# Attention over 16 heads: the causal mask and the row maximum in one VectorE operation, the copy of the values on ScalarE

## The reference, cut to what matters

```python
K = jnp.einsum('bpd,ihd->biph', x, W_K)            # 16 heads of 64
Q = jnp.einsum('bpd,ihd->biph', x, W_Q)
V = jnp.einsum('bpd,ihd->biph', x, W_V)
scores = jnp.einsum('biph,biqh->biqp', K, Q)
mask = jnp.tril(jnp.ones((q_len, q_len), dtype=bool))
scores = jnp.where(mask[None, None, :, :], scores, NEG_INF)
attn = jax.nn.softmax(scores / np.sqrt(d_head).astype(np.float32), axis=-1)
z = jnp.einsum('biph,biqp->biqh', V, attn)
out = jnp.einsum('bqf,df->bqd', z_flat, W_O)
```

## Time and profile before

| | us |
|---|---|
| median of 3 runs | 565.84 (563.9 to 568.18) |
| the profiled execution, its time | 566.51 |
| its span in the profile | 564.7 |

### The profile page before, as it was taken

How to read it: one execution, slowest core, us unless ns; L and a number is a source line. 1 busy time by engine, 2 the same in 40 slices (tenths; PEclk the granted TensorE clock), 3 DMA queues, 4 the chain that set the end, 5 groups by cost and what they waited for, 6 DMA issues and landing times.

```text
span 564.7 us, 10428 instructions
## 1 busy us (share of the span) xinstructions
PE 461.5 (82%) x3500; PEld 362.5 (64%) x3500; DVE 374.8 (66%) x1091; ACT 228.8 (41%) x835; POOL 235.9 (42%) x245
## 2 busy tenths in 40 slices
PE   3957895715989179999999999999999997419993
PEld 2324554614989046777787877878787785319993
DVE  6598976851666347767768687696777955345772
ACT  2720001501444006555646466366564564104451
POOL 5002784471444314433435334363444624322453
PEclk9987998555999669999999999999999999758998
DMA  8999600034464200000000000000000000116560
GB/s 296 403 422 420 277 1 1 15 109 136 142 176 148 77 1 2 1 1 2 1 1 2 2 1 11 11 20 1 2 11 11 21 0 1 39 62 178 155 201 19
DMA packets 21878, 47.73 MB, mean 85 GB/s; under 512 B 3233, under 2 KB 13480, under 8 KB 19394
## 3 DMA queue, kind: packets, MB, share of 16 engines
q1 hardware_dynamic: 18818, 40.73, 20.7%
q0 software_dynamic: 3008, 6.34, 3.3%
HBM read 23.82 MB, written 24.15 MB: 85 GB/s over the span
## 4 chain that ended last, share of the span: by engine, by line
PE 69%; DVE 10%; POOL 8%; DMA 5%; issue 5%; ACT 2%; POOLq 0%; SPq 0%; ACTq 0%; DVEq 0%
PE ps L888 10%; PE ps L917 9%; PE ps L964 8%; PE ps L951 7%; PE ps L833 7%; PE ps L846 6%; PE ps L905 5%; PE ps L895 5%; PE ps L923 3%; POOL sum L441 3%; DMA pv<-in_w 2%; POOL sorted_in L466 2%; PE ps L681 2%; POOL sum L445 2%; PE ps L787 1%
## 5 line engine op out<-in xcount | busy, mean ns | idle before, releaser
L495 POOL TENSOR_TENSOR vT<-vT,prec 128x256 f32<-128x256 f32 (+1 forms) x128 | 103.1, 825 | 157.5 <-DVE prec L1373 157.4
L632 ACT ACTIVATE vT<-ps,nmax 128x128 f32<-128x128 f32 (+1 forms) x256 | 105.1, 434 | 27.8 <-DVE nmax L1365 27.8
L640 ACT COPY prod<-ps 128x384 f32<-128x384 f32 x96 | 42.9, 481 | 111.3 <-PE ps L951 108.3
L1365 DVE TENSOR_REDUCE nmax<-ps 128x2 f32<-128x256 f32 (+1 forms) x128 | 62.3, 548 | 25.6 <-PE ps L923 25.6
L888 PE MATMUL ps<-xnT,wb 128*128 128x256 f32 x256 | 67.9, 389 | 4.6 <-DVE xnT L1345 3.9
L951 PEld LDWEIGHTS ps<-cst,vT 128*128 128x128 f32 x384 | 44.7, 140 | 18.8 <-issue 14.5
L632 ACT ACTIVATION_READ_ACCUMULATOR vT<-ps,nmax 128x1 f32 x256 | 55.9, 218 | 0.0
L951 PE MATMUL ps<-cst,vT 128*128 128x128 f32 x384 | 52.5, 273 | 1.8 <-POOL vT L495 1.7
L888 PEld LDWEIGHTS ps<-xnT,wb 128*128 128x128 f32 x256 | 44.8, 195 | 10.8 <-DVE xnT L1345 4.3
L917 PE MATMUL ps<-qk 64*128 64x128 f32 (+1 forms) x512 | 51.2, 339 | 0.0
L964 PE MATMUL ps<-prod 128*64 128x256 f32 (+1 forms) x512 | 50.0, 338 | 1.4 <-ACT prod L640 1.4
(11 more groups left out here) (152 smaller groups left out, 829.8 us busy)
## 6 DMA issues: line engine op xcount, KB each, us to landing
sorted_in<-zero SPq DMA_DIRECT2D x1, 16512.0 KB, 59.2
pv<-in_w SPq DMA_DIRECT2D x30, 259.0 KB, 2.8
pv<-sorted_in SPq DMA_DIRECT2D x46, 129.0 KB, 2.5
wps<-in_w SPq DMA_DIRECT2D x1, 2072.0 KB, 10.1
w2s<-in_w SPq DMA_DIRECT2D x1, 2048.0 KB, 13.8
wb<-in_w_b SPq DMA_DIRECT2D x1, 1536.0 KB, 18.0
xres<-in_x SPq DMA_DIRECT2D x4, 256.0 KB, 3.6
xres<-after_ffn SPq DMA_DIRECT2D x4, 256.0 KB, 3.8
```

Of the source, the lines that this page charges most:

```text
L495: last = nc.gpsimd.tensor_tensor(px, px, view(prec, m_at(n, x) + t * 2, [[1, 2], [0, (t + 1) * P]]), ALU.mult)
L632: last = nc.scalar.activation(pb[:, o:o + (t + 1) * P], wide[:, c:c + (t + 1) * P], ACT.Exp, bias=nmax[:, m:m + 1], accum_out=psum[:, m:m ...
L640: nc.scalar.copy(pT[:, c:c + BLOCKS * P], bank[hh][:, 0:BLOCKS * P]).then_inc(b_pa, 1)
L1365: last = nc.vector.tensor_reduce(nmax[:, m:m + 2], view(wide, x * 1024 + t * P, [[512, 2], [1, (t + 1) * P]]), AX.X, ALU.max, negate=True)
```

## The change

The mask matmuls and their bf16 constants go. VectorE's reductions become eight fused operations, `tensor_tensor_reduce`: each reads one score block from PSUM and the mask from `cst` in SBUF, writes -(scores + mask) back in place and gives the minimum of that, which is `nmax`. The exponential reads with scale -1. The mask has a block of zeros (`C_OPEN`) ahead of its triangle (`C_CAUSAL`), so that one piece of 256 columns serves `t = 1`. `b_s` now counts once for a step, behind the scores of both pairs, and VectorE waits for it ahead of `invert(n, 1)`. `copy_v` goes from VectorE to ScalarE, between `copy_p(n, 1, 1)` and `exp_b(n1, 1)`. VectorE's `copy_p` stands ahead of the last fused operation, and `copy_qk(n2, 0)` ahead of the last four.

```diff
@@ constants @@
-C_ID, C_BEFORE, C_CAUSAL, C_FIRST, C_UPTO = 0, 128, 256, 384, 392
+C_ID, C_BEFORE, C_OPEN, C_CAUSAL, C_FIRST, C_UPTO = 0, 128, 256, 384, 512, 520
@@ ScalarE @@
-            nc.scalar.copy(id_bf[:], ident)
...
-            nc.scalar.copy(causal[:], cst[:, C_CAUSAL:C_CAUSAL + P]).then_inc(in_r, 1)
...
-                                                    bias=nmax[:, m:m + 1], accum_out=psum[:, m:m + 1])
+                                                    bias=nmax[:, m:m + 1], scale=-1.0, accum_out=psum[:, m:m + 1])
...
+            def copy_v(n, i):
+                act.wait_ge(b_vp, nth(n) + 3)
+                c = (i % 2 * HB + i // 2 * 8) * DHB
+                nc.scalar.copy(vb[:, c:c + 8 * DHB], bank[2][:]).then_inc(b_v, 1)
...
                 if ok(n):
                     copy_p(n, 1, 1)
+                if some(bv) and j != 1 or some(b) and j == 1:
+                    copy_v(n, (j + 2) % STEPS)
                 if ok(n1):
                     exp_b(n1, 1)
@@ TensorE: mask_b is gone, scores_b signals @@
+                if x == 1:
+                    last.then_inc(b_s, 1)
...
                     scores_b(n1, 1)
-                    mask_b(0)
                 if ok(n):
                     turn_p(n, 0)
-                if ok(n1):
-                    mask_b(1)
@@ VectorE @@
-            def max_b(n, x):
-                dve.wait_ge(b_s, 2 * nth(n) + x + 1)
-                for t in range(T):
-                    m = m_at(n, x) + t * 2
-                    last = nc.vector.tensor_reduce(nmax[:, m:m + 2],
-                                                   view(wide, x * 1024 + t * P, [[512, 2], [1, (t + 1) * P]]),
-                                                   AX.X, ALU.max, negate=True)
-                last.then_inc(b_mx, 1)
+            def scored(n):
+                dve.wait_ge(b_s, nth(n) + 1)
+
+            def max_b(n, x, hh, t):
+
+                m, c, open_at = m_at(n, x) + t * 2 + hh, (2 * x + hh) * 512 + t * P, C_CAUSAL - t * P
+                s = wide[:, c:c + (t + 1) * P]
+                ins = nc.vector.tensor_tensor_reduce(out=s, in0=s, in1=cst[:, open_at:C_CAUSAL + P], scale=-1.0,
+                                                     scalar=-MASKED * 2, op0=ALU.add, op1=ALU.min,
+                                                     accum_out=nmax[:, m:m + 1])
+                if hh and t:
+                    ins.then_inc(b_mx, 1)
...
                 if ok(at(b, j - 1)):
                     copy_z(at(b, j - 1))
+                if ok(n1):
+                    scored(n1)
                 if ok(n):
                     invert(n, 1)
                 if ok(n1):
-                    max_b(n1, 0)
-                    max_b(n1, 1)
+                    for hh in range(2):
+                        for t in range(T):
+                            max_b(n1, 0, hh, t)
                 if ok(n2):
                     copy_qk(n2, 0)
-                if some(bv) and j != 1 or some(b) and j == 1:
-                    copy_v(n, (j + 2) % STEPS)
+                if ok(n1):
+                    max_b(n1, 1, 0, 0)
+                    max_b(n1, 1, 0, 1)
+                    max_b(n1, 1, 1, 0)
                 if ok(n):
                     copy_p(n)
                 if ok(n1):
+                    max_b(n1, 1, 1, 1)
                     invert(n1, 0)
```

More of the change, by code:

```diff
@@ L243, in hybrid_layer @@
         wob = sb("wob", [P, NPAIR * D])
-        id_bf = sb("id_bf", [P, P], BF16)
-        causal = sb("causal", [P, P], BF16)
         qk = sb("qk", [P, RING * 2 * L])
@@ L550, in _ @@
             nc.scalar.copy(before[:], cst[:, C_BEFORE:C_BEFORE + P])
-            nc.scalar.copy(id_bf[:], ident)
-            nc.scalar.copy(region[:], cst[0:1, C_REGION:C_REGION + GT * NE])
-            nc.scalar.copy(causal[:], cst[:, C_CAUSAL:C_CAUSAL + P]).then_inc(in_r, 1)
+            nc.scalar.copy(region[:], cst[0:1, C_REGION:C_REGION + GT * NE]).then_inc(in_r, 1)
             turned(0)
@@ L640, in copy_p @@
                 nc.scalar.copy(pT[:, c:c + BLOCKS * P], bank[hh][:, 0:BLOCKS * P]).then_inc(b_pa, 1)
+            def copy_v(n, i):
+                act.wait_ge(b_vp, nth(n) + 3)
+                c = (i % 2 * HB + i // 2 * 8) * DHB
+                nc.scalar.copy(vb[:, c:c + 8 * DHB], bank[2][:]).then_inc(b_v, 1)
             def step(b, j):
                 n, n1 = (b, j), at(b, j + 1)
+                bv = b + j // 2
                 if ok(n):
@@ L660, in _ @@
             act.wait_ge(f_sent, NT * 16)
-            all_steps(step, 1, 0)
+            all_steps(step, 3, 0)
             residual(1, NG - 1)
@@ L916, in scores_b @@
                         c = (2 * x + hh) * 512 + t * P
[L917 to L926, removed]
+                        last = nc.tensor.matmul(wide[:, c:c + (t + 1) * P], qk[rows, r + t * P:r + (t + 1) * P],
+                                                qk[rows, r + L:r + L + (t + 1) * P],
+                                                start=t == 0, stop=t == T - 1, skip_group_check=True)
+                if x == 1:
+                    last.then_inc(b_s, 1)
             def turn_p(n, x):
@@ L1336, in norm_b @@
                 last.then_inc(b_xn, 1)
[L1338 to L1341, removed]
             def copy_xT(b):
```

## The result

The changed kernel takes 561.91 us in the median of 19 runs, the kernel before 565.84 in 19: 3.9 us less, where 7.5 was forecast. The ratio estimated from all these runs is 0.9915, with 0.9892 to 0.9937 as the 95% interval (the quotient of the two medians is 0.993). So the change makes the kernel faster by less than 1%, which is clear of the noise but only about half of the 1.3% forecast. The profiled execution took 561.05 us with a span of 559.2.

What follows compares the result with a forecast made beforehand. PE was taken to bound attention b, with values_b waiting in three steps of four after the change. Eight batches -8.2, opening +0.5, constants +0.2: -7.5 us, from 565.84 to 558.3; range 551 to 579.

Steps and rivals of the forecast that it cites:

- The forecast start of values_b: In a plain step, after ACT's copy of the values: 4.40 + 2A = 5.86 us, where PE wants to start at 5.41.
- The price of a head, A: On DVE, a 128 and a 256 fused operation with their accumulator reads: 0.73 us, bounds 0.55 and 1.01.
- The 0.77 worked out from its table: A estimated from the skill page's cycles per operation (120 from PSUM, 58 from SBUF): batch 32.7 us, 561 us in all.
- The way from ACT's copy back to PE: Semaphore time between the end of ACT's copy of the values and the start of values_b: 0.05 us.
- The mask: Mask matmuls on PE, 0.32 + 0.22 = 0.54 us in each of 32 steps, 17.3 us in all.
- A batch: Four steps of attention b, 3 x 7.31 + 10.55 = 32.48 us against 33.51: 1.03 less, 8.2 over eight batches.
- the reciprocal, whose later start the prediction priced at nothing: DVE's invert(n, 1), at 1.65 instead of 0.65 us: pair 1's weights ready at 3.41, turn_p(n, 1) due at 3.89.
- The opening: Start of attention b, first maxima on DVE: about 1.0 us more for eight fused operations, less 0.54 of mask, +0.5.
- the 0.2 for the longer constants: Load of constants 64 KB longer, behind the first piece of x: 0.2 us taken, bound 0 to 0.9.
- full length: Rival: fused operations and reads run end to end, A = 1.01, +13.7, 579.5 us; chance 0.23, with near cases and the clock.
- PE stays the bound: Rival: reads hide wholly or values_b needs less, nearly all 0.54 a step gained, -16.6, 549 us; chance 0.08.
- in between: Rival: fused operation or read takes up to 0.08 more, A 0.77 to 0.9, 561 to 570 us, no change; chance 0.28.

Runs made afterwards that it cites:

- dve_delay: Kernel after with one more VectorE operation, a 128x128 copy of constants, ahead of each step's first fused operation: 564.27 us, 0.997 of the kernel before.
- pair_signal: Kernel after with b_s counted for each pair, so VectorE starts with the first pair's scores: 557.91 us, 0.984 of the kernel before.
- wait_order: Kernel after with the four waits of values_b reordered, the one for the copy of the values last: 562.23 us, one run.
- pe_no_mask: Kernel before with its mask matmuls left out and no causal mask applied in attention b: 557.32 us, 0.985 of the kernel before.
- copy_v_dve: Kernel after with the copy of the values back on VectorE, ahead of its copy of the weights: 570.89 us, 1.006 of the kernel before.

## Why the prediction was half right

The path was the one predicted: scores, reciprocal, fused operations, four exponentials, two copies on ACT, values_b; three steps of four wait and the output step doesn't. dve_delay lengthens it and pair_signal shortens it, and the output steps without routing stay at 10.70 in both. The forecast start of values_b, 5.86 after the scores, is 266.69 - 260.82 = 5.87 in the trace. That hit is partly luck, since its terms missed on both sides:

- The price of a head, A, was put at 0.73 and is 0.63. The accumulator read costs the next instruction hardly anything: 2A is 0.20 less. The upper bound of 1.01, instructions at full length one after the other, is far off. The page "VectorE: DVE Perf Modes" of the Trainium skill says in "The DRAIN you can't avoid" that the next operation waits until the pipe is empty, and also, which the prediction left out, that one that is not held starts earlier. This trace agrees with the second: the next one starts together with the read, 0.14 ahead of the read's recorded end. The 0.77 worked out from its table was too high as well (and by the prediction's own sum it gives 560 us from the median; 561 counts from the profiled execution).
- The way from ACT's copy back to PE was put at 0.05, the value of a PE to DVE wait. It is 0.25 (wait_order: 0.11 of that by the order of the waits), and values_b takes 1.52 after a wait and not 1.45: 0.27 more.
- So a waiting step is 7.39 and not 7.31: 0.08 in 24 steps by the prediction's count, 1.9 us. In fact 20 steps wait, as dve_delay shows: the prediction took all eight batches for the same and left out the routing.
- The mask was put at 0.54 of PE's time and is 0.39 (pe_no_mask), since the transposes take 0.14 longer when they come first behind the scores. In the waiting steps this was hidden; in the eight output steps it is 10.70 and not 10.55, 1.2 us.

A batch was to be 32.48 and is 3 x 7.39 + 10.70 = 32.87, which is 0.64 below the 33.51 of before: 5.1 us in all instead of 8.2. In the trace the stretch of values_b is 4.5 us shorter (258.7 to 254.3); two of the three output steps with routing work grew from 11.42 to 11.65, as they do in pe_no_mask (11.75), and hold part of the rest. In the first of these the chain leaves PE and runs through DVE's routing work, `copy_z` (377.11), the reciprocal (377.71) and GpSimd's divide (377.88 to 379.50) to the second six transposes. So the reciprocal, whose later start the prediction priced at nothing, stands on the chain there, and in no plain step.

The opening, forecast at +0.5, can't be read from these traces. From the start of the stage's first work on DVE (201.82 before, 200.98 after) to the first values_b (220.00 and 219.06) it is 18.2 and 18.1 us. But TensorE's granted clock is 0.50 at its start and rises to 1.00 within it, at about 208 us in the kernel before, 206 in the kernel after and 204 in dve_delay, whose opening takes 17.5 us although it has one operation more in each step than the kernel after. Of the 0.2 for the longer constants no run shows anything either, against first stages that move by more.

The step of the prediction that failed is thus the return from ACT to PE, put at 0.05 and measured at 0.25, with the 0.07 that values_b takes longer after a wait, together with the size of the mask, put at 0.54 and measured at 0.39. Both are waits and covers between engines, not the price of the new operation, which I had taken for the only unknown.

Of the rivals, "full length" and "PE stays the bound" are out by the trace. The case "in between", 561 to 570, held the measured time, which lies outside the 556 to 560 of the forecast, but not by its mechanism: A is below the forecast's, not above. The point where the gain is used up was put at A = 0.83; with the prediction's own terms, the late output step included, it is 0.85. The clock stayed at 1.00 from the first values_b on to 460 us, with the new gaps in PE.

The larger question is what became of the mask's removal. On PE alone it shortens the stretch of values_b by 9.9 us (pe_no_mask, 258.7 to 248.8), and the change keeps 4.5 of them. The other 5.4 went into the wait of values_b. Most of it comes back with one thing undone, the merged signal: `scored(n1)` makes DVE wait for both pairs' scores, 0.75 us longer than the first pair needs. Counted for each pair again it gives back 3.7 (254.3 to 250.5), and with the waits in order 1.3 more, to 249.2.

## What to carry to other kernels

When work is taken off the engine that bounds, walk one step of the loop from a fixed point through every engine, with distances between starts and not recorded lengths, and look for the wait that ends closest ahead of the bound: before the change the last copy that values_b needs ended 0.27 us ahead of it (275.19 + 0.56, against 276.02). A signal that is merged to save a wait delays everything behind it, and an order of waits in which the last to be satisfied stands last costs nothing. Where small work is removed, look at what stands behind it: it may have taken a cost that its successor takes now, as the transposes take 0.14 here.

## What the runs showed of the hardware that was not expected

DVE's accumulator read behind a fused operation is recorded with 142 ns, yet the next operation on DVE starts with it. A 128x256 operation with a PSUM and an SBUF input that writes back to PSUM and reduces takes 0.38 us from start to start, 0.04 more than the same columns at the spacing of plain reductions.

PE starts 0.25 us after a copy on ACT has ended when a satisfied wait stands behind that one, and 0.14 when it is the last (wait_order, and the first values_b of the kernel after). It starts 0.09 after a copy on DVE (copy_v_dve), at the first values_b, which has no wait for `b_z`, as at the later ones, which have. So what holds behind ACT doesn't hold behind DVE; why stays open.

The first six transposes behind the scores take 0.80 to 0.81 us in the chain, six others 0.66. The scores have 64-row weights and the transposes 128-row ones; whether that change takes the 0.14 wasn't taken apart.
